# Delta-rule mixer on one Trainium2 core: two gate products between the key placements, and a 4-fold copy for the state seed

## The reference

```python
q, k, v = (silu(short_conv(h @ W)) for W in (Wq, Wk, Wv))    # h = layernorm(x); 16 heads of 16
beta = sigmoid(h @ Wb)
q, k = l2norm(q) * 0.25, l2norm(k)
def step(S, inp):                      # S: 16 x 16 per batch and head, 512 steps
    u = vt - einsum('bhk,bhkv->bhv', kt, S)
    S = S + beta_t * outer(kt, u)
    return S, einsum('bhk,bhkv->bhv', qt, S)
o = rmsnorm(o) * sigmoid(h @ Wg)       # the gate
x = x + o @ Wo
```

## Time and profile before

| | |
|---|---|
| median of 3 runs | 845.69 us (845.59 to 847.47) |
| the profiled execution's own time | 841.79 us |
| its span | 840.0 us |
| its mean granted TensorE clock | 0.994 |
| TensorE busy | 786.3 us |
| VectorE busy | 482.3 us |
| ScalarE busy | 361.3 us |
| GpSimd busy | 218.0 us |

### The profile page before, as it was taken

How to read it: one execution, slowest core, us unless ns; L and a number is a source line. 1 busy time by engine, 2 the same in 40 slices (tenths; PEclk the granted TensorE clock), 3 DMA queues, 4 the chain that set the end, 5 groups by cost and what they waited for, 6 DMA issues and landing times.

```text
span 840.0 us, 14393 instructions
## 1 busy us (share of the span) xinstructions
PE 786.3 (94%) x4825; PEld 544.4 (65%) x4825; DVE 482.3 (57%) x1166; ACT 361.3 (43%) x756; POOL 218.0 (26%) x318
## 2 busy tenths in 40 slices
PE   5988799879989998899999999989999999999998
PEld 3576566666657785677777767766764545455557
DVE  5999866766522225866565565767755463324443
ACT  3988767646123333352332342323246676211111
POOL 3644654111610034111111111116712233200000
PEclk9998999999999999999999999999999999999999
DMA  4001780092343322034442322212333433294431
GB/s 144 2 1 31 231 292 2 2 229 79 107 144 102 101 69 68 21 104 121 144 131 68 101 68 68 76 39 92 113 82 114 134 95 116 73 289 127 126 126 50
DMA packets 95807, 85.72 MB, mean 102 GB/s; under 512 B 34792, under 2 KB 84456, under 8 KB 95736
## 3 DMA queue, kind: packets, MB, share of 16 engines
q1 hardware_dynamic: 88200, 70.05, 28.7%
q0 software_dynamic: 4224, 11.74, 4.1%
q10 hardware_dynamic: 3312, 3.02, 1.1%
HBM read 57.02 MB, written 26.71 MB: 100 GB/s over the span
## 4 chain that ended last, share of the span: by engine, by line
PE 75%; DVE 10%; ACT 7%; issue 4%; DMA 1%; POOL 1%; SPq 0%; ACTq 0%; another core or an unknown queue 0%; DVEq 0%; POOLq 0%
PE bank L1488 9%; PE bank L1451 7%; PE bank L1306 6%; PE bank L1345 6%; PE bank L1267 6%; PE bank L1283 6%; PE bank L1331 5%; PE bank L730 4%; PE bank L756 3%; PE bank L953 3%; PE bank L2309 3%; PE bank L975 2%; ACT arena L2366 2%; PE bank L2266 2%; PE bank L2293 2%
## 5 line engine op out<-in xcount | busy, mean ns | idle before, releaser
L1607 ACT ACTIVATE arena<-bank 128x512 f32<-128x512 f32 (+1 forms) x96 | 46.9, 525 | 147.4 <-PE bank L1451 135.2
L1229 POOL TENSOR_TENSOR arena<-arena,causal_t 128x256 f32<-128x256 f32 x64 | 45.2, 726 | 215.9 <-ACT arena L1612 215.9
L1488 PEld LDWEIGHTS bank<-arena 128*128 128x128 f32 x640 | 76.1, 191 | 4.8 <-POOL arena L1229 3.5
L1488 PE MATMUL bank<-arena 128*128 128x129 f32 x640 | 77.2, 275 | 1.9 <-POOL arena L1229 1.9
L1451 PE MATMUL bank<-arena 128*128 128x512 f32 (+3 forms) x256 | 74.6, 434 | 1.4 <-DVE arena L1685 1.4
L1540 ACT ACTIVATE arena<-bank 128x512 f32<-128x512 f32 (+1 forms) x39 | 20.2, 520 | 123.3 <-PE bank L1267 106.9
L1306 PE MATMUL bank<-arena 128*128 128x256 f32 (+1 forms) x272 | 66.2, 382 | 4.4 <-DVE arena L1665 2.7
L1267 PE MATMUL bank<-xnT,arena 128*128 128x512 f32 (+1 forms) x168 | 65.9, 514 | 0.0
L1306 PEld LDWEIGHTS bank<-arena 128*128 128x128 f32 (+1 forms) x272 | 50.9, 190 | 22.6 <-issue 13.2
L1345 PE MATMUL bank<-arena 128*128 128x256 f32 x256 | 61.0, 381 | 2.5 <-DVE arena L1692 2.0
L1345 PEld LDWEIGHTS bank<-arena 128*128 128x128 f32 x256 | 48.1, 190 | 23.3 <-issue 12.0
(11 more groups left out here) (296 smaller groups left out, 1486.7 us busy)
## 6 DMA issues: line engine op xcount, KB each, us to landing
arena<-in_w_gu SPq DMA_DIRECT2D x44, 256.0 KB, 3.3
rows_in<-place SPq DMA_DIRECT2D x5, 1664.0 KB, 14.4
arena<-in_w_dn SPq DMA_DIRECT2D x34, 128.0 KB, 3.5
rows<-arena SPq DMA_DIRECT2D x8, 544.0 KB, 4.3
arena<-in_w_dn SPq DMA_DIRECT2D x24, 176.0 KB
arena<-in_wq SPq DMA_DIRECT2D x32, 128.0 KB
arena<-in_wo SPq DMA_DIRECT2D x32, 128.0 KB
arena<-rows SPq DMA_DIRECT2D x32, 128.0 KB, 2.1
```

The lines of the kernel that those rows point to most:

```text
L1229: nc.gpsimd.tensor_tensor(blocks, blocks, causal_t[:].unsqueeze(1).to_broadcast([P, 2, P]), ALU.mult).then_inc(s_p, 1)
L1488: mm = nc.tensor.matmul(b_o[pair][:, t * (DH + 1):(t + 1) * (DH + 1)], pr[:, o:o + P], v[:, grp, kt, :], start=(kt == 0), stop=(kt == qb))
L1607: nc.scalar.activation(th[:, sbank * 512:sbank * 512 + w], b_s[sbank][:, 0:w], ACT.Tanh, scale=SCALE / SOFTCAP).then_inc(s_th, 1)
```

## The change

On TensorE, `gates(0)` is issued ahead of key placement 3 and `gates(1)` ahead of placement 5, in place of behind turn 2. `gates(2)`, `gates(3)`, all the turns and all of ScalarE's stream keep their place. On GpSimd, the four copies of each head into `seed` become one copy of 32 x 4 x 16 whose source is repeated by a stride of zero.

```diff
@@ pe(self, pe) @@
+            def gates(i):
+                if i == 0:
+                    pe.wait_ge(s_siv, KD + 4)
+                if i >= 2:
+                    pe.wait_ge(s_ge, i - 1)
+                for j in range(2):
+                    n = 2 * i + j
+                    for k in range(KD):
+                        mm = nc.tensor.matmul(bank[i % 2][:, j * DIM:(j + 1) * DIM], xnT[:, k, n * P:(n + 1) * P],
+                                              w0[:, G_, k, :], start=(k == 0), stop=(k == KD - 1), skip_group_check=True)
+                mm.then_inc(s_g, 1)
+
             pe.wait_ge(s_one, 1)
             for u in range(8):
+                if u in (3, 5):
+                    gates((u - 3) // 2)
                 if u == 0:
                     pe.wait_ge(s_uz, 10)
...
             turn_ft(1)
             turn_ft(2)
-            gates(0)
-            gates(1)
             turn_ft(3)
             gates(2)
             turn_ft(4)
...
@@ pool(self, pool) @@
             for h in range(4):
                 rows = slice(32 * h, 32 * h + 32)
                 nc.gpsimd.memset(hdiag[rows, h, :], 1.0)
-                for x in range(4):
-                    ins = nc.gpsimd.tensor_copy(seed[rows, x * 64 + h * D0:x * 64 + (h + 1) * D0],
-                                                ident[rows, 32 * h + D0:32 * h + 32])
+                ins = nc.gpsimd.tensor_copy(seed[rows].rearrange("p (x h d) -> p x h d", x=4, d=D0)[:, :, h, :],
+                                            ident[rows, 32 * h + D0:32 * h + 32].unsqueeze(1).to_broadcast([32, 4, D0]))
```

More of the change, by code:

```diff
@@ L2210, in pe @@
             pe.wait_ge(s_kqe, 8)
[L2212 to L2222, removed]
             def turn_ft(i):
```

## The result

| | before | changed |
|---|---|---|
| median | 845.98 us (843.89 to 847.57, 8 runs) | 849.76 us (848.04 to 852.83, 8 runs) |
| the profiled execution's own time | 841.79 us | 848.75 us |
| its span | 840.0 us | 846.9 us |
| its mean granted TensorE clock | 0.994 | 0.986 |

The ratio is 1.0047, with a 95% interval of 1.0028 to 1.0066: the change costs 2.4 to 5.6 us. That is slower by more than the 2.5 us that the prediction took as its bound, inside the stated range, and above the 847.3 that it named. The prediction gave this side 0.19 and "no change" 0.76.

What follows compares the result with a forecast made beforehand. It took VectorE's solve as floor, with TensorE's stream and ScalarE's turn copies ending 0.6 us behind. The gates(2) wait's +1.6 us and 0 for the seed copies, on a median of 845.69, gave 847.3, range 844.0 to 850.4.

Steps and rivals of the forecast that it cites:

- The bound of the stretch: First mixer's preparation: VectorE's solve sets the floor; TensorE's stream, gates(3), its sigmoid and ScalarE's turn copies also set the end.
- the prize of 0.6 us: End of the first mixer's preparation: a faster TensorE could bring the last `ft_out` at most 0.6 us earlier.
- TensorE 3.3 us later at turn 0: Placements: two gate groups cost 3.8 us, less 0.46 of idle time filled, so turn 0 starts 3.3 us later.
- The new wait: gates(2) on TensorE waits for group 0's sigmoid on ScalarE, over 2 us idle, and starts 1.6 us later.
- Behind that the stream is as before, at full clock: From gates(2) on, TensorE runs at full clock as before, so the last `ft_out` ends at 93.5, not 91.90.
- rival 2: Clock stays at half for gates(2) and what follows: 3.3 to 6.7 us, 849.0 to 852.4; chance 0.18.
- moves whole: Behind the last `ft_out`, the chain over the chunks follows and shifts by the same +1.6 us.
- The prediction's own sign: It is wrong if the distance from the last `ft_out` to the span's end changes by over 1 us.
- Rival 1: TensorE's clock does not fall in the sums, gates(2) starts 0.1 us late, result 845.8; chance 0.22.
- The table load: ScalarE ahead of group 0's sigmoid: the table switch takes 1.28 us, without the skill's added drain of about 1.38 us.
- The edges at no cost: Later `qx` transfers, weight loads and `wz`, and fewer seed copies, cost or gain nothing; solve at most 0.2 us, taken as 0.

Runs made afterwards that it cites:

- four fillers: The changed kernel with four extra products nobody reads on TensorE ahead of gates(2); 847.73 us, ratio 1.0035.
- early sigmoids: The changed kernel with ScalarE's sigmoids of gate groups 0 and 1 moved ahead of its turn copies 1 and 2; 845.85 us, ratio 1.0011.
- gates alone: Against the changed kernel, the seed copies put back as before, so only the gates move; 850.65 us, ratio 1.0076.
- two fillers: The changed kernel with two extra 128x256 products nobody reads on TensorE ahead of gates(2); 848.83 us, ratio 1.0058.
- change once more: The full change, unaltered, measured again beside the other kernels on one chip; 849.40 us, ratio 1.0045.
- seed copies alone: Against the kernel before, only GpSimd's copies into `seed` merged, the gates where they were; 846.26 us, ratio 1.0019.
- kernel with the tail: The kernel with early sigmoids, with turns 5 and 6 ahead of gate group 3 on both engines; 845.69 us, ratio 1.0008.
- gates among the sums: Against the kernel with the tail, gate groups 0 and 1 go behind the sums' first and second halves, none among the placements; 846.02 us, ratio 0.9999.

## Why the prediction was right or wrong

**The bound of the stretch: right.** The floor by VectorE's solve and the prize of 0.6 us held: the best order tried won 0.44 us, and then VectorE was last.

**TensorE 3.3 us later at turn 0: right.** It is 77.21 - 61.66 = 15.55 us after L2192, against 72.86 - 60.72 = 12.14: 3.4 us. Only the gap ahead of placement 5 was filled, as the prediction said.

**The new wait: right, its term a little too large.** gates(2) starts 25.53 us after L2192 and not 24.22: 1.3 us late, where the term said 1.6. The clock fell later into the sums, so they took 4.55 us and not 4.99, which gave ScalarE its turn copies sooner. The idle time of 2.27 us ahead of it was foretold as over 2.

**"Behind that the stream is as before, at full clock": this step failed.** gates(2) took 3.41 us to the next turn where it took 1.73 (87.19 to 90.60, against 84.94 to 86.67). That is 1.7 us more, and 1.3 + 1.7 = 3.0 us at the last turn copy: its end comes 34.14 us after L2192, against 31.18. It was the prediction's rival 2, with the hole ahead of gates(2) as its place, 1.7 us as its price, and 3.3 us or 849.0 as its result, at a chance of 0.18. It should have been the likeliest case: in all three profiled executions of this order gates(2) ran at the lower clock. The forecast copied how long the clock had stayed low before, although it said itself that the work which had raised the clock was what the change took away. The four fillers show the step: with the hole filled the clock rises by 88 and gates(2) takes 1.89 us. With the early sigmoids half speed by itself costs nothing: there gates(2) took 3.57 us too, but started 3.0 us sooner.

**From the last turn copy on: not quite "moves whole".** The 3.0 us at the last turn copy are 2.7 at the first product of the chain and 3.5 at L2345, and the 0.5 between 3.0 and 3.5 go with the second low stretch, which the prediction doesn't have (0.3 with the gates alone, 0.5 with two fillers, which have it too). In the change once more, which has no second one, 4.6 us stand at all three places. Why the clock falls there was not tried. Half clock in the first stretch cost 1.7 us, the late wait 1.3, the second stretch 0.5: with them the median's 3.6 to 3.8 us are nearly accounted for.

The prediction's own sign, over 1 us of change from the last `ft_out` to the span's end, came true: 748.1 us before, 751.1 in the changed kernel. Beside those 0.5 us, about 1.6 us each went near 251 and 561, at the lower clock. The kernel with the seed copies alone has two such places too (mean granted clock 0.67 in 248 to 252, 0.73 in 556 to 560), and its products there are the kernel before's. So the change isn't needed for them. Between 110 us and the last 10 us of the span the profile before has no such place at all, while the nine others have one to four each (2 to 4 in the five with the order of the change, fillers or not, 1 to 3 in the other four). The profiled execution before was one of the quickest of its kernel, 4.2 us under the median. Whether the change makes such places more frequent was not tried.

**Rival 1, the clock doesn't fall: wrong, in all nine executions profiled after the prediction.** TensorE had no hole from 66.64 to 76.2 in the changed kernel, then one of 0.96 us ahead of turn 0, and the clock fell at 80.1, some 2.4 us into the sums. The Trainium skill (TensorE: Matmul & The Clock Gate, "Why this matters for your kernels") advises against long idle gaps between bursts of matmuls. The trace shows that this isn't enough: from 61.66 to the fall no idle time of TensorE was over 1.14 us, and the clock fell all the same. Filling the placements was no help; whether the 0.96 us or the narrow sums brought the fall stays open.

**The table load: the row was right.** The sigmoid began at 86.54, 1.30 us after the start of its load at 85.24. The drain of some 1.38 us that the Trainium skill adds (ScalarE: Activation LUTs, "What ACT_TABLE_LOAD costs") doesn't show on this load either, although it is on the critical chain now.

**The edges at no cost: right.** The seed copies' gain became idle time. The transfers into `qx` moved to 81.12 and were issued by 91.2, with their reader at 101. The solve was untouched: it ends 29.3 us after L2192 in both.

## What to carry to other kernels

Products that are issued 13 us earlier are worth nothing if the engine that empties their bank still does so at its old place in its order, since every later user of that bank waits for that place: move the two together. Where work is moved out of a stretch of low clock, ask what TensorE will do there afterwards, because behind a hole of 2.3 us in it the next group took 3.6 to 3.8 us here and not 1.9. And when executions differ by more than a change is worth, compare a stretch between two marks in one engine's stream: two kernels lay 0.01 us apart there whose medians could not be told apart to 2 us. Two cautions go with that: the end mark has to lie behind everything that the change moves (0.8 us came behind the first one here), and a stretch with low clock in it varied by 1.9 us between two executions of one kernel.

## What the runs showed of the hardware

- The granted clock fell while TensorE was continuously busy, in all ten executions profiled, 2.0 to 3.0 us behind the start of the sums, in nine of them during products 8 columns wide. An idle time of 0.95 to 0.98 us that ended 2.5 to 3.5 us before the fall is common to all, and no run parts the two. Gate products set between the halves of the sums did not prevent the fall (it came in the first of them), and the clock stayed at 0.50 for 10.2 us there, with no hole.
- It rose again only behind a run of products 128 or 256 columns wide without a hole. With 1.9 us of fillers and then 0.55 us idle it did not rise ahead of gates(2); with no idle time at all it did, within 3.0 us of the fillers' start. From the start of the gate products that preceded the rise it took 1.9 us in the kernel with the tail and 5.7 in the change once more.
- Around the sums the low stretch lasted 6.8 us in five executions, all without a hole in it. With a hole it lasted 10.2 us (the changed kernel, the gates alone, the two fillers) and 13.7 us (the change once more); with the gates among the sums it had no hole and lasted 10.2 us.
- GpSimd's copies of 32 x 64 with a repeated source took 0.23 to 0.62 us each; those of 32 x 16 took 0.19 to 0.66. So a copy of four times the elements costs about as much.
